# A four-layer graph kernel: two weight products by seven block products, shorter target spans, and degrees from summed counts

## What is computed

```python
# layer 0: adj = 0/1 matrix with both directions of each edge, + I; D = row sums
x = LN(x + D^-1/2 adj D^-1/2 (x @ W0) + b0)
# layer 1: A[s, d] = number of edges s -> d, + I; dinv = (column sums)^-1/2
for W, b in ((W1, b1), (W2, b2), (W3, b3)):
    h = dinv * (A^T @ (dinv * (h @ W))) + b       # h = x at first
x = LN(x + h)
# layer 2: attention over the 0/1 matrix of edges, q, k, v = x @ W + b
x = LN(x + softmax(mask(q @ k^T / sqrt(512))) @ v)
# layer 3: two convolutions as in layer 1, relu between them
h = relu(dinv * (A^T @ (dinv * (x @ V1))) + c1)
x = LN(x + dinv * (A^T @ (dinv * (h @ V2))) + c2)
```

## Time and profile before

| what | value |
| --- | --- |
| median of 3 runs | 561.21 us (561.19 to 561.22) |
| profiled execution: time | 561.48 us |
| profiled execution: span, first to last instruction | 559.7 us |
| TensorE busy | 548.4 us, 98% of the span |
| VectorE busy | 341.6 us, 61% |
| ScalarE busy | 168.5 us, 30% |
| GpSimd busy | 128.8 us, 23% |
| mean granted TensorE clock | 0.997 |

### The profile page before, as it was taken

How to read it: one execution, slowest core, us unless ns; L and a number is a source line. 1 busy time by engine, 2 the same in 40 slices (tenths; PEclk the granted TensorE clock), 3 DMA queues, 4 the chain that set the end, 5 groups by cost and what they waited for, 6 DMA issues and landing times.

```text
span 559.7 us, 6522 instructions
## 1 busy us (share of the span) xinstructions
PE 548.4 (98%) x2137; PEld 340.9 (61%) x2137; DVE 341.6 (61%) x770; ACT 168.5 (30%) x361; POOL 128.8 (23%) x128
## 2 busy tenths in 40 slices
PE   8999999999999999999999999999999999999995
PEld 6655456457788645888864764544454686468643
DVE  6989899896578644335586975947384600540165
ACT  5998796482021321210130000412132102210200
POOL 3000000065036303022125710750500430000022
PEclk9999999999999999999999999999999999999998
DMA  8723000010140010000000000000050000000012
GB/s 292 254 77 132 19 0 1 5 36 1 39 145 8 0 19 1 0 1 0 3 1 0 0 1 0 2 0 0 1 169 0 2 0 0 1 0 1 0 56 96
DMA packets 11432, 19.09 MB, mean 34 GB/s; under 512 B 2171, under 2 KB 2435, under 8 KB 11398
## 3 DMA queue, kind: packets, MB, share of 16 engines
q1 hardware_dynamic: 11398, 18.63, 9.8%
HBM read 16.52 MB, written 2.11 MB: 33 GB/s over the span
## 4 chain that ended last, share of the span: by engine, by line
PE 85%; DVE 8%; issue 3%; DVEq 3%; POOL 0%; POOLq 0%; ACT 0%
PE bank L718 16%; PE bank L700 16%; PE bank L770 14%; PE bank L888 13%; PE bank L910 10%; PE bank L884 4%; DVE count L1226 4%; PE bank L597 3%; PE bank L593 3%; DVE hot_key L1210 2%; DVEq L1218 1%; PE bank L900 1%; PE bank L628 1%; PE bank L605 1%; DVE lo_near L1204 1%
## 5 line engine op out<-in xcount | busy, mean ns | idle before, releaser
L486 POOL TENSOR_TENSOR rstd<-veps,mhalf 128x1 f32<-128x1 f32 x32 | 22.7, 710 | 213.5 <-DVE veps L1300 210.6
L910 PE MATMUL bank<-vv,probt 128*128 128x512 f32 x128 | 56.1, 592 | 0.0
L770 PE MATMUL bank<-v_sb,gt 128*128 128x512 f32 (+1 forms) x136 | 55.3, 567 | 0.0
L1226 DVE TENSOR_TENSOR count<-bank,count 128x192 f32 x128 | 45.7, 357 | 11.4 <-PE bank L628 6.2
L718 PE MATMUL bank<-adj,y_hi 128*128 128x512 f32 x128 | 51.3, 401 | 0.0
L718 PE MATMUL bank<-adj,y_lo 128*128 128x512 f32 x128 | 50.5, 395 | 0.0
L1307 DVE SCALAR_TENSOR_TENSOR xs<-bank,dinv,xs 128x512 f32<-128x512 f32 x23 | 17.0, 749 | 49.7 <-PE bank L770 37.2
L983 ACT ACTIVATE apart<-col_lo,edge_key 128x128 bf16<-128x128 int16 x128 | 43.9, 394 | 0.9 <-PE bank L617 0.9
L770 PEld LDWEIGHTS bank<-v_sb,gt 128*128 128x128 f32 x136 | 25.8, 190 | 28.8 <-issue 27.7
L910 PEld LDWEIGHTS bank<-vv,probt 128*128 128x128 f32 x128 | 23.9, 190 | 27.7 <-issue 27.7
L1210 DVE TENSOR_TENSOR hot_key<-col_key,key 128x384 bf16<-128x384 int16 x128 | 39.7, 351 | 0.1
(11 more groups left out here) (216 smaller groups left out, 1089.6 us busy)
## 6 DMA issues: line engine op xcount, KB each, us to landing
w_sb<-in_L_gnn_W_dram SPq DMA_DIRECT2D x3, 1024.0 KB, 5.6
xs<-in_x_dram SPq DMA_DIRECT2D x2, 1024.0 KB, 7.1
v_sb<-in_L_gnn_W_dram SPq DMA_DIRECT2D x2, 1024.0 KB, 6.7
out_dram<-xs SPq DMA_DIRECT2D x7, 256.0 KB, 2.0
w_sb<-in_L_gnn_weight_dram SPq DMA_DIRECT2D x4, 256.0 KB, 5.9
wq_sb<-in_L_gnn_Wq_dram SPq DMA_DIRECT2D x1, 1024.0 KB, 10.7
wk_sb<-in_L_gnn_Wk_dram SPq DMA_DIRECT2D x1, 1024.0 KB, 12.6
wv_sb<-in_L_gnn_Wv_dram SPq DMA_DIRECT2D x1, 1024.0 KB, 7.7
```

Of the source, the lines that this page charges most:

```text
L486: nc.gpsimd.tensor_tensor(rstd[:, j:j + 1], veps[:, j:j + 1], mhalf[:, j:j + 1], ALU.pow).then_inc(rstd_set, 1)
L770: mm = pe.matmul(bank[:, 0 if cols is high_cols else HALF * (s % 2) + b, cols], g(k, j), w[:, k, cols], start=k == 0, stop=k == FB - 1)
L910: mm = pe.matmul(bank[:, 6 + m % 2, :], probt[:, m % 2, j, :], vv[:, j, :], start=j == 0, stop=j == NB - 1)
L1226: return V.tensor_tensor(count[:, :, bass.ds(at_dst, WIN)], bank[:, slot, n * KEYS:(n + 1) * KEYS].rearrange("p (h d) -> p h d", h=NB), co ...
```

## The change

- `WIN` goes from 24 to 20: 160 columns for 192 in the count, 320 elements for 384 in `hot_key`.
- The column sums of the counts are taken on VectorE by three additions (`fours`, `twos`, `col_sums`) between its `low` instructions of step 0, and TensorE sums over partitions in two float32 products instead of 16 float32r ones.
- The inverse roots are written to memory (`dinv_kept`) and read back as a row on all partitions (`dinv_row1`, `dinv_row`). VectorE multiplies the turned aggregates by it (`scaled_cols`), in place of ScalarE's copies, after its dot products.
- The products with `wfold` (kind "f") and V1 (kind "h") are made by 14 parts each, as "v". VectorE makes `gt1_sums` and `gt_sums` and adds up the results; biases and splits are fitted in between. The adjacency steps behind them take the blocks in the order `PAIRS`.
- `wq_rows` is loaded early, in the place of Wv; Wv is loaded after the "f" parts. `wk_rows` stays where it was, but the write of `dinv_kept` and the wait for it now stand ahead of it on SP's queue.

```diff
-WIN = 24
+WIN = 20
...
-            sp.dma_start(wv_sb[:], wview(wv)).then_inc(w_in["v"], 16)
+            sp.dma_start(wq_rows[:], wview(wq)).then_inc(wqk_in, 16)
...
+            sp.wait_ge(dinv_set, 1)
+            sp.dma_start(dinv_kept[0, :].rearrange("(j p) -> p j", p=P), dinv[:, 1, :],
+                         allow_slow_non_contiguous=True).then_inc(dinv_out, 16)
+            sp.wait_ge(dinv_out, 16)
             sp.wait_ge(hs_done, 2 * HALF)
             sp.dma_start(wk_rows[:], wview(wk)).then_inc(wqk_in, 16)
-            sp.dma_start(wq_rows[:], wview(wq)).then_inc(wqk_in, 16)
+            sp.dma_start(dinv_row1[:], dinv_kept[0, :].partition_broadcast(P)).then_inc(dinv_in, 16)
...
+            pool.wait_ge(unit_out, NU)
+            pool.wait_ge(dots_set, 2 * FB + 1)
+            left_sums(wfold, three(f_sums), f_summed)
+            pool.wait_ge(part_done, FOLDED)
+            left_sums(mfold, three(m_sums), m_summed)
...
+            def degree_row(first):
+                pe.wait_ge(cols_set, 1)
                 for half in range(2):
-                    for k in range(NB):
-                        mm = pe.matmul(bank[0:2, first + half, :], ones2[:], mat[:, k, half * D:(half + 1) * D],
-                                       start=k == 0, stop=k == NB - 1)
+                    mm = pe.matmul(bank[0:2, first + half, :], ones[:, 0:2], col_sums[:, half * D:(half + 1) * D],
+                                   start=True, stop=True)
...
                 cols_steps(2, adj, yb, NB, more)
-                for half in range(2):
-                    weight_step(4 + half, half, lambda k, j: gt1[:, j, k, :], wfold, 2 + half)
-                for s, y, lo_from in ((6, ya, 2 * NB), (8, yb, 3 * NB)):
-                    for half in range(2):
-                        rows_step(s + half, adj, y, lo_from, more)
+                for n in range(FOLDED):
+                    part(*PARTS[n])
+                for half in range(2):
+                    rows_step(4 + half, adj, ya1, 2 * NB, more, order=PAIRS)
+                for half in range(2):
+                    rows_step(6 + half, adj, yb1, 3 * NB, more)
...
+                if h == HALF:
+                    dve.wait_ge(sym_max, NB)
+                    then(V.tensor_tensor(fours[:], count[:, 0:HALF, 0:N], count[:, HALF:NB, 0:N], ALU.add))
+                if h == HALF + 1:
+                    then(V.tensor_tensor(twos[:], fours[:, 0:2, :], fours[:, 2:HALF, :], ALU.add))
+                    V.tensor_tensor(col_sums[:], twos[:, 0, :], twos[:, 1, :], ALU.add).then_inc(cols_set, 1)
...
+            def scaled_cols(s, to, by):
+                for half in range(2):
+                    cols = slice(half * D, (half + 1) * D)
+                    for f in range(FB):
+                        dve.wait_ge(hs_done, (s + half) * HALF + f + 1)
+                        V.tensor_tensor(to[:, f, cols], bank[:, HALF * half + f, :], by[:, cols], ALU.mult).then_inc(dve_out, 1)
...
+            dve.wait_ge(dinv_in, 16)
+            scaled_cols(2, gt1, dinv_row1)
+            right_sums(gt1, gt1_sums, gt1_summed, 3)
+            m2("f", 0)
+            m2("f", 1)
...
+            for n in range(2):
+                for step in (m6, m7, m5, m3):
+                    step("f", n)
+                fold_at(4 * n)
+                fold_at(4 * n + 1)
+                fold_low(4 * n)
+                m4("f", n)
+                fold_at(4 * n + 2)
+                fold_low(4 * n + 1)
+                fold_at(4 * n + 3)
+                fold_low(4 * n + 2)
+                fold_low(4 * n + 3)
```

More of the change, by code:

```diff
@@ L161, in gnn_kernel @@
         biasc2 = bias0
-        fold1 = sb("fold1", [P, D], F32)
-        fold2 = sb("fold2", [P, D], F32)
+        at_folds = region(3 * D * 4)
+        fold1 = at("fold1", at_folds, [P, D], F32)
+        fold2 = at("fold2", at_folds + D * 4, [P, D], F32)
         grow = fold2[0:2, :]
-        urow = sb("urow", [P, D], F32)
+        urow = at("urow", at_folds + 2 * D * 4, [P, D], F32)
+        v1_sums = at("v1_sums", at_folds, [P, 3, 2, D // 2], F32)
+        wv_sums = (at("wv_sums1", at_folds, [P, 2, D // 2], F32)[:],) + tuple(
+            at("wv_sums" + str(n), r2 + 7 * N * 4 + n * D * 4, [P, 2, D // 2], F32)[:] for n in range(2))
+        wide = at("wide", r1 + 2 * W, [P, NB, D], F32)
+        gt_sums = at("gt_sums", r2 + 2 * W, [P, 3, 2, D], F32)
+        dinv_row = at("dinv_row", r2 + 2 * W + 3 * 2 * D * 4, [P, N], F32)
+        dinv_kept = nc.dram_tensor("dinv_kept", [1, N], F32, kind="Internal").ap()
         ident = sb("ident", [P, P], F32)
@@ L543, in _ @@
                 nc.gpsimd.tensor_tensor(xs[:, j, :], xs[:, j, :], biasc2[:], ALU.add).then_inc(biased, 1)
+            pool.wait_ge(w_in["v1"], 16)
+            left_sums(v1_sb, three(v1_sums), v1_summed)
             inverse_roots(3 * NB, 4 * NB)
@@ L682, in _, with rows_step @@
                     piece(m)
-            def rows_step(s, mat, y, lo_from, more=None, before={}):
-                for k in range(NB):
-                    if k in before:
-                        before[k]()
-                    pe.wait_ge(lo_set, lo_from + k + 1)
+            def rows_step(s, mat, y, lo_from, more=None, before={}, order=range(NB)):
+                for n in range(NB):
+                    k = order[n]
+                    if n in before:
+                        before[n]()
+                    pe.wait_ge(lo_set, lo_from + n + 1)
                     if s < 2:
@@ L1093, in first_part @@
                 nc.scalar.copy(block_of(of, n, "C12"), as_rows(of, bank[:, bank_of((of, n, "M1")), :])).then_inc(act_parts, 1)
+            act.wait_ge(*freed(3, HALF - 1))
+            first_part("f", 0)
+            first_part("f", 1)
+            for m in range(NB):
+                act.wait_ge(folded, m + 1)
+                high(ya1, PAIRS[m], rows_a[:, PAIRS[m], :])
+            for k in range(NB):
+                act.wait_ge(*freed(4 + k // HALF, k % HALF))
+                high(yb1, k, rows_b[:, k, :])
             def exponents(m):
@@ new lines, in _ @@
+            for n in range(2):
[10 more added lines that the diff above has]
+                fold_low(4 * n + 3)
+            for k in range(NB + 1):
+                if k < NB:
+                    dve.wait_ge(hs_done, 4 * HALF + k + 1)
+                    V.scalar_tensor_tensor(out=rows_b[:, k, :], in0=bank[:, k, :], scalar=dinv[:, 1, k:k + 1], in1=fold1[:],
+                                           op0=ALU.mult, op1=ALU.add).then_inc(dve_out, 1)
+                if k >= 1:
+                    low(3 * NB + k - 1, yb1, rows_b[:, k - 1, :], dinv[:, 1, k - 1:k])
@@ L1445, in row_terms @@
+            for j in range(NB):
+                if j == HALF:
+                    normalise(NB + HALF - 1)
+                residual(NB + j, 6 + j // HALF, NB + j + 1, 1)
+                if j % HALF:
+                    normalise(NB + j - 1)
+            normalise(2 * NB - 1)
             def row_terms(first, last):
```

311 lines of the change are left out of this document (170 added, 141 removed).

## The result

The changed kernel takes **548.97 us** (median of 4 runs, 547.77 to 549.56) where the kernel before takes 561.20 in the same session (561.01 to 561.22): a ratio of 0.978, interval 0.9762 to 0.9798. Forecast were 549.6 us. The profiled execution took 549.56 us, with a span of 547.8 and a clock of 0.999; it is the slowest of the four, 0.6 us above their median.

The account below looks back on a forecast made before the run. TensorE, busy 98% of the span, was taken to bound the kernel. Savings of 5.1 (counting), 1.8 (degrees), 1.4 (wfold) and 3.3 (V1) sum to 11.6 us, from 561.2 to 549.6 us; range 546.6 to 554.0.

Parts of the forecast that it names:

- Counting: Count stage with 20 targets a span: fewer columns and fewer TensorE waits save 5.1 us.
- Rival (3): Counting gains only its gaps, or as little, because ScalarE holds the pace: 2.0 for 5.1 us, total 552.7; chance 0.09.
- Rival (5): A second round of counting, 64 groups more, some 87 us slower; chance 0.03 together with unknown.
- Degrees: Row of degrees: two float32 products replace 16 matmuls on TensorE, 1.8 us less, nothing late.
- Rival (2): VectorE's 16-bit sums run at 1.03 ns an element: 3 us worse, total 552.6; chance 0.08.
- Product with wfold: Layer 1's product in 14 parts: 3.3 us less, minus a 1.9 us gap at its start, net 1.4.
- rival (1): The write of the inverse roots takes no longer than u_rows: 1.5 us better, total 548.1; chance 0.28.
- rival (4): The scattered write of inverse roots is much slower: 33 us cancels the gains, 45 gives some 573; chance 0.04.
- Product with V1: The product with V1 in 14 parts: 24.2 us for 27.46, 3.3 us less.
- Nothing late behind the parts: Behind the wfold parts, VectorE's sums, biases and lows come in time for step 4; no size given.
- The adjacency steps and attention as before: The profile would show these stages unchanged; no term in the sum.
- all bounds bad: Every term at its worst bound: total 555.6 us.

Follow-up runs that it names:

- w24: The changed kernel with spans of 24 targets again instead of 20, all else as changed: 554.85 us, ratio 0.9878.
- w16: The changed kernel with spans of 16 targets instead of 20, so the counts are gone through twice: 630.35 us, measured once.
- hold4: The changed kernel with the inverse roots written four times, each write waited for, ahead of the load of wk_rows: 573.17 us, ratio 1.0216.
- v1_eight: The changed kernel with the product with V1 made by eight block products as before: 551.62 us, ratio 0.9828.
- bias_late: The changed kernel with GpSimd's eight layer-bias additions moved behind the left sums for attention: 549.72 us, ratio 0.9788.
- noelse: The changed kernel without the untaken second-matrix version of the code in layers 1 and 3: 547.34 us, ratio 0.9744.
- w18: The changed kernel with spans of 18 targets instead of 20: 548.84 us, ratio 0.9771.
- shift24: The changed kernel with 24 empty instructions ahead of TensorE's first wait: 549.98 us, ratio 0.979.
- deg_old: The changed kernel with column sums by 16 float32r matmuls on TensorE again, without VectorE's three sums: 549.29 us, ratio 0.9776.
- best_swap: The changed kernel with padding to 256 bytes behind the counts, 18 targets a span, and the branches exchanged so the taken one stands last: 552.95 us, ratio 0.9857.
- pad256: The changed kernel with everything behind the counts moved up to a multiple of 256 bytes from the adjacency tensor: 546.86 us, ratio 0.9735.

## Why the prediction was right, point by point

- **Counting: right, 5.1 for 5.23.** `w24` gives it back; that it does so to the hundredth is chance, as the starts of step 0 in nine kernels with 20 targets are spread over 1.0 us. The parts hold as well: comparisons 316 ns and additions 323 (forecast 317 and 325), waits for `hot_key` 0.6 for 2.4. TensorE's gaps fell by 1.6 us, where 2.0 less 0.6 was forecast, which leaves 3.6 to the columns for 3.7. ScalarE did become full from 14 to 42 us; that it took the 0.6 us set aside for it fits the sum, and was not measured by itself. Rival (3) is out. Rival (5), excluded for 20 targets by the distance of 17, is what `w16` showed: 81 us where 87 were worked out.
- **Degrees: right, 1.8 for 1.88**, of which 0.19 is lost again in the matmuls right behind, a cost that the prediction left out: 1.7 net. The 16-bit sums took 4.0 us for the first two where the rate of comparisons gives 3.3, and 1.37 for the third. Rival (2) is out: VectorE waited for the row.
- **Product with wfold: the term that was mis-sized.** "If the wait grows with the numbers, it is 20 us" does not hold: 7.4 us for 1024, 8.5 for 2048. So `wk_rows` left at 161.29, at the end of step 1, and the gap was 0.2 us for 1.9, by the route of rival (1). Against that the chain has the parts at 24.44 us for 24.2. Net 3.03 - 0.21 = 2.8 us for 1.4. The mechanism, order and price of lateness, was right: `hold4` made the write late by force, and what rival (4) named came, the wait for VectorE, the fall of the clock and some 573 us, at 42 us of writing for the 45 of the estimate.
- **Product with V1: right, 3.3 for 3.29**, and `v1_eight` takes exactly that back.
- **Nothing late behind the parts: right.** No wait of TensorE stands in them or in steps 4 to 7, but there is no room either: `bias_late` shows that a microsecond more on each low part is felt at once.
- **"The adjacency steps and attention as before": wrong by three terms.** Steps 4 to 7 gained 0.87 us by the place of their operands, steps 10 to 13 lost 0.27 (with 24 targets as well, so not by the place that the span sets; the cause is open), and the gap in turning x cost 1.7 net. Together they took 1.1 us (1.88 - 0.18 + 0.27 - 0.87) of the 13.0 that the named terms made. With the wait sized rightly, the forecast by its own terms would have been rival (1)'s 548.1; the unnamed terms brought the time back to 549.0. The forecast came nearer than its mis-sized term deserved, which is luck.
- **A slip in a bound.** With all bounds bad the prediction's own terms give 2.0 - 1.2 + 1.4 + 2.3 = 4.5 us, so 556.7 and not 555.6. The chances and the range do not use it.

The Trainium skill (DMA: Bandwidth & Descriptors, section on the anatomy of one DMA) has some 2 us as the fixed cost of a transfer, mostly the receipt; its figure is for transfers issued through GpSimd, and those here are SP's. As to the growth with count it was the better guide here; as to size the traces disagree with it for single numbers, 8.8 to 11.2 us from issue to landing in the chain of `hold4`.

**The gap at the tenth transpose.** Shown is that it goes with the jump: absent without the second branch (`noelse`), moved to the head of layer 1 with the branches exchanged, there with 1.1 to 2.0 us in ten of the eleven kernels that keep the order, the changed one among them. In the changed kernel one 16 KB instruction transfer begins at 267.4 us, 0.6 us ahead of the gap, and in `noelse` none lies there (the next is at 270.6 us). In all ten, TensorE goes on 1.2 to 1.5 us after the end of such a transfer, so the gap is long where the transfer ends late. In `w24`, `w18` and `shift24` the profile puts the same gap down to VectorE's L1384 (L1386 in `shift24`), the normalising of a row of x; `deg_old` rules that out, since its transposes are done by 270.0 us and that instruction (L1381 there) starts at 270.53. The Trainium skill (Runtime: NRT & Kernel Launch, section on instruction fetch mechanics) says that a taken branch to a target outside the blocks at hand forces a fetch before the engine can go on. The traces agree in place and in kind for the jump of layer 1, not for that of layer 3 in `best_swap`. Open is what decides whether there is a gap. `deg_old` and the kernel before keep the jump and have no gap, with transfers at 265 and 268 us in `deg_old`; both have other numbers of instructions for TensorE ahead of the jump, while 24 more in `shift24` changed nothing. Of the 7.0 us in `best_swap`, 4.0 are its one long transfer; why that one was long, and what the other 3.0 are, is open. That the code's place relative to the fetched blocks decides is argued, not shown.

**The operands' place.** Shown by `pad256` and `best_swap`, and four spans fit one account: what lies behind the counts is off a multiple of 256 bytes from `adj` by 0 bytes with 16 targets or the pad, 64 with 20, 128 with 24 and 32 with 18 (8 rows of 2 x (1024 + `WIN`) bytes), and steps 4 to 7 took 58.07, 58.61, 59.48 and 59.73 us. The kernel before, with 24, has 59.48 as well, and `w24` has it with the changed order of blocks, so the order is not the cause. The pad alone was tried against 64 and 32 bytes (`pad256`, and `best_swap` beside `w18`, the latter with the branches exchanged as well); 128 rests on the spans. Steps 0 and 1, whose two operands both lie behind the counts and move together, take 12.73 or 12.74 us for their first 56 matmuls in all fourteen kernels: it is the place of one operand relative to the other that counts. So 0.87 us of the change's gain is a by-product of a constant that was altered for another reason, and `w18` lost 1.1 us in the same way.

## What to carry to other kernels

Move a stage and read the stage: three of twelve runs (`w18`, `deg_old`, `bias_late`) moved their own stretch as forecast and the total hardly, since a gap or a slower stretch elsewhere took it; the chain, start against start, tells such a case from a change that does nothing. One profile of each is not exact: the same stretch (up to step 0, with 20 targets) differs by up to 1.0 us between kernels that do not differ there. Where a kernel's arrays are resized, keep the operands of its long matmul loops at the same place to 256 bytes from one another, or measure with a pad: here it was worth 2.1 us for one line. And code that is never run can cost: in layer 1 it cost 10 us ahead of the path that is taken (one kernel), behind it 1.1 to 2.0 in ten kernels and nothing in two, absent nothing; so leave it out where it can be proved idle, and otherwise look at the first microseconds behind each jump.

## What the runs showed of the hardware that was not expected

- A write of single 4-byte numbers to memory takes 8.1 to 11.2 us from issue to landing, whether there are 512, 1024 or 2 x 1024 of them.
- The same float32r matmuls of 128x128 by 128x512 go at 227, 229, 232 or 233 ns, start to start, with the place of their operands in SBUF relative to each other.
- A VectorE instruction with two operands in SBUF takes 1.76 us beside GpSimd's two-operand adds and 0.68 alone, while its 16-bit sums ran at 0.62 ns an element against 1.03 ns for sums out of PSUM.
- TensorE stood 1.1 to 2.0 us ten transposes behind a jump, and went on 1.2 to 1.5 us after a 16 KB instruction transfer had ended, in ten kernels; in another arrangement it stood 7.0 us two matmuls behind a jump, with a transfer of 4.0 us in it.
